# Relation stage: two chunks a step, rows stacked by the kind of the source node

## The reference

```python
h = jnp.maximum(_layernorm(x, axis=-1), 0.0)
# weight: 8 bases of 64 x 64; w_comp: 16 relations x 8 bases
# relation of an edge = (edge type, kind of source, kind of target): 4 * 2 * 2
# out[dst] += h[src] @ (sum over b of w_comp[relation, b] * weight[b]);  + bias
x = x + _L2_gnn_ref(h, node_type_2, src, dst, edge_type_4, weight, w_comp, bias)
```

## Time and profile before

| what | value |
|---|---|
| median of 3 runs | 9735.94 us (9728.96 to 9739.63) |
| profiled execution | 9729.18 us, span 9727.4 us |
| VectorE, TensorE, GpSimd, ScalarE busy in the span | 72%, 64%, 46%, 28% |
| relation block, first gather to the end of its block | 6232.5 to 7149.5 us |

### The profile page before, as it was taken

One profiled execution on the slowest core, in us unless ns is written; L12 is line 12 of the kernel. 1 busy time (PEld: TensorE's weight loads), 2 busy tenths in 40 slices (PEclk: granted clock), 3 DMA queues, 4 the chain that ended last, 5 costly groups with the idle time before them and its releaser, 6 DMA issues. The chain is left out here.

```text
span 9727.4 us, 105611 instructions
## 1 busy us (share of the span) xinstructions
PE 6247.1 (64%) x15818; PEld 3037.1 (31%) x15818; DVE 6982.1 (72%) x21830; ACT 2708.9 (28%) x6469; POOL 4476.3 (46%) x4367
## 2 busy tenths in 40 slices
PE   0006999996999996774001998899979999900000
PEld 0002333333444444663000556533323333300000
DVE  2666887785666666886556997799979999887522
ACT  0002333331111112554332000122224444346300
POOL 1775555554555553554552000144446666413466
PEclk9998555555666665555555995699965555555555
DMA  4002334342222221112332004444433333323222
GB/s 144 1 1 42 56 55 57 56 55 48 47 47 47 47 47 25 38 36 55 89 89 57 3 1 124 123 100 101 100 73 74 75 73 75 72 93 111 83 81 79
DMA packets 937155, 627.22 MB, mean 64 GB/s; under 512 B 639609, under 2 KB 801942, under 8 KB 935568
## 3 DMA queue, kind: packets, MB, share of 16 engines
q1 hardware_dynamic: 579396, 305.26, 12.3%
q0 software_dynamic: 137984, 138.92, 10.9%
q10 hardware_dynamic: 219656, 181.82, 5.7%
HBM read 431.05 MB, written 227.84 MB: 68 GB/s over the span
## 5 line engine op out<-in xcount | busy, mean ns | idle before, releaser
L707 POOL DMA_INDIRECT a_xg<-t_XL,a_ix x784 | 790.0, 1008 | 688.2 <-issue 653.2
L707 POOL DMA_INDIRECT b_xg<-t_H,b_ix x784 | 776.6, 991 | 666.6 <-PE b_bank L917 378.5
L1737 POOL DMA_INDIRECT f_dg<-t_D,f_ix x392 | 370.6, 945 | 1498.2 <-DMA f_ix<-t_PSRC 1402.2
L707 POOL DMA_INDIRECT g_xg<-t_D,g_ix x784 | 824.0, 1051 | 493.4 <-issue 225.5
L1090 POOL DMA_INDIRECT t_RANK<-m_place,m_at x392 | 385.6, 984 | 409.0 <-DMA m_place<-t_POS 301.8
L1275 POOL DMA_INDIRECT l_d<-t_D,l_ix x392 | 370.7, 946 | 405.4 <-DVE l_xs L1291 238.0
L1365 PE MATMUL pr_prow<-c_ident,pr_col 128*1 128x128 f32 x2 | 0.6, 396 | 789.9 <-DVE pr_col L1383 789.9
L2135 POOL DMA_INDIRECT out<-o_y,o_ix x392 | 388.8, 992 | 225.4 <-issue 184.3
L428 POOL DMA_INDIRECT t_XL<-ix_pv,ix_si x392 | 407.9, 1041 | 159.4 <-issue 130.3
L745 DVE TENSOR_TENSOR b_zt<-b_xl,b_bank 128x512 f32<-128x512 f32 x98 | 67.4, 687 | 537.4 <-PE b_bank L936 237.3
L1324 ACT ACTIVATE l_hn<-l_xs,l_sm 128x64 f32<-128x64 f32 x784 | 265.0, 426 | 505.6 <-DVE l_sm L588 283.9
(11 more groups left out here) (437 smaller groups left out, 17260.9 us busy)
## 6 DMA issues: line engine op xcount, KB each, us to landing
t_XL<-in_nodes ACTq DMA_DIRECT2D x10, 2578.1 KB
t_XSD<-a_xg SPq DMA_DIRECT2D x98, 256.0 KB
t_H<-a_oE ACTq DMA_DIRECT2D x98, 256.0 KB
l_xb<-t_XSD SPq DMA_DIRECT2D x49, 512.0 KB
f_rl<-t_REL SPq DMA_DIRECT2D x98, 256.0 KB
g_xb<-t_XSD SPq DMA_DIRECT2D x98, 256.0 KB
n_x<-in_x SPq DMA_DIRECT2D x39, 640.0 KB
out<-n_y ACTq DMA_DIRECT2D x39, 640.0 KB
```

The costliest lines, as they stand in the source:

```text
L707: nc.gpsimd.indirect_dma_start(xg[k][:, j, i, :], None, table, bass.IndirectOffsetOnAxis(ap=ix[k][:, i, j:j + 1], axis=0)).then_inc(s_g[k] ...
L1737: nc.gpsimd.indirect_dma_start(dg[k][:, j, :], None, T["D2"], bass.IndirectOffsetOnAxis(ap=ix[k][:, j:j + 1], axis=0)).then_inc(s_g[k], 16)
```

## The change

A step takes two chunks, 1024 edges, and there are 49 (`NB`). The kind of the source node is told apart by rows: `positions_block` no longer adds it to the number of the relation but stores it as T["KS"]. norm splits scale and shift into two pairs, one multiplied by the kind, the other by one less the kind (`by_kind`); normed then writes each row twice, once in columns 0 to 63 and once in 64 to 127, and the ReLU leaves zeros in the half that isn't the edge's. Turned, that is 128 rows. The two kinds' weights lie above each other in c_wft, so f_v takes two products of 128 rows for 512 edges where it took four of 64, and f_sel and f_m come in twos as well. The four banks of f_v now hold two halves of a step, f_m has one bank for each half, and turn and turn back keep one bank each: both halves pass through the one turn bank in turn.

Loads, gathers, sums, copies and norm factors are of 1024 edges, with four slots for what comes in up to f_hn and two for the rest. VectorE's list is result 5, select 3, sums 4, norm 1. TensorE's is vectors of the first half 3, compose of the first half 4, the same for the second half, turn 2, turn back 4. SyncE's relations have lag 2. The diff, cut to its core; of a function changed throughout only the new lines stand, since the old ones are printed above:

```diff
-            n += load(C["wflat"][:, :, :], a["L2_gnn_weight"].rearrange("b i o -> (b i o)").rearrange("(q p i) -> p q i", p=P, i=D))
+            for q in range(4):
+                n += load(C["wflat"][:, q % 2, q // 2, :],
+                          a["L2_gnn_weight"].rearrange("b i o -> (b i o)").rearrange("(q p i) -> q p i", p=P, i=D)[q])
...
+            sp.dma_start(full(T["KS"]), ks[:, :]).then_inc(s_st, 16)
+            sp.wait_ge(s_st, 32)
...
-            ch(v.scalar_tensor_tensor(part[:, :], kind[0][:, :], 8.0, et[:, :], ALU.mult, ALU.add))
-            v.scalar_tensor_tensor(rel[:, :], kind[1][:, :], 4.0, part[:, :], ALU.mult, ALU.add).then_inc(s_done, 1)
-            ch.done()
+            v.tensor_copy(ks[:, :], kind[0][:, :])
+            v.scalar_tensor_tensor(rel[:, :], kind[1][:, :], 4.0, et[:, :], ALU.mult, ALU.add).then_inc(s_done, 1)
...
-            for q in range(4):
-                last = nc.tensor.transpose(pf[:, q, :], C["wflat"][:, q, :], C["ident"][:, :])
+            for q in range(2):
+                last = nc.tensor.transpose(pf[:, q, :], C["wflat"][:, q, :, :].rearrange("p c i -> p (c i)"), C["ident"][:, :])
...
+        SL = 4
+        NB = NCH // 2
+        G = 2 * J
+        four, two = range(SL), range(2)
+        hn = [m.sb(f"hn{k}", [P, 2, J, 2, D]) for k in four]
+        hT = [m.sb(f"hT{k}", [P, 2, CH]) for k in two]
+        rl = [m.sb(f"rl{k}", [P, 2, CH]) for k in two]
...
+        by_kind = m.sb("bykind", [P, 2, 2, G])
         b_turn = m.ps("turn", [P, CH])
+        b_v = [[m.ps(f"v{u}{g}", [P, CH]) for g in two] for u in two]
+        b_m = [m.ps(f"m{u}", [P, CH]) for u in two]
+        b_back = m.ps("back", [P, 2, J, D])
...
+                    sp.wait_ge(s_g[k], 16 * G * q)
+                sp.dma_start(ix[k][:, :, :], words_of_two(T["PSRC"], n)).then_inc(s_ix[k], 16)
+                if old:
+                    sp.wait_ge(s_f, n - SL + 1)
+                for u in two:
+                    sp.dma_start(xb[k][:, u, :, :], rows_of_two(T["XSD"], n)[:, u, :, 0:D]).then_inc(s_xb[k], 16)
+                sp.dma_start(ks[k][:, :, :], words_of_two(T["KS"], n)).then_inc(s_xb[k], 16)
...
+                if later(n, 2):
                     sp.wait_ge(s_sel, 4 * (n - 1))
...
+                    sp.wait_ge(s_ag, 2 * (n - 1))
...
-            flow(sp, [(0, load), (4, before), (3, keeps), (1, relations)])
+            flow(sp, [(0, load), (4, before), (3, keeps), (2, relations)], total=NB, slots=SL)
...
+                for u in two:
+                    for j in range(J):
+                        nc.gpsimd.indirect_dma_start(
+                            dg[k][:, u, j, :], None, T["D2"],
+                            bass.IndirectOffsetOnAxis(ap=ix[k][:, u, j:j + 1], axis=0)).then_inc(s_g[k], 16)
+            flow(pool, [(0, gather)], total=NB, slots=SL)
...
+                dve.wait_ge(s_g[k], 16 * G * (q + 1))
+                dve.wait_ge(s_xb[k], 48 * (q + 1))
+                if old:
+                    dve.wait_ge(s_hn, n - SL + 1)
+                v.tensor_tensor(xs[k][:, :, :, :], dg[k][:, :, :, :], xb[k][:, :, :, :], ALU.add).then_inc(s_xs, 1)
                 dve.wait_ge(s_xs, n + 1)
+                ch(row_moments(nc, flat(xs[k][:, :, :, :]), bn))
+                norm_factors(nc, ch, bn, sm, s_n)
+                dve.wait_ge(s_n, n + 1)
                 if later(n):
                     dve.wait_ge(s_hn, n)
+                of_source = ks[k][:, :, :].rearrange("p u j -> p (u j)").unsqueeze(1).to_broadcast([P, 2, G])
+                ch(v.tensor_tensor(by_kind[:, 1, :, :], sm[:, 4:6, :], of_source, ALU.mult))
+                v.tensor_tensor(by_kind[:, 0, :, :], sm[:, 4:6, :], by_kind[:, 1, :, :], ALU.subtract).then_inc(s_f, 1)
                 ch.done()
...
+                dve.wait_ge(s_rl[k % 2], 16 * counted(n, k, q))
+                for u in two:
+                    if later(n, 2):
+                        dve.wait_ge(s_m, 2 * (n - 2) + u + 1)
+                    for g in two:
+                        dve.wait_ge(s_v, 4 * n + 2 * u + g + 1)
+                        v.scalar_tensor_tensor(sel[k % 2][u][g][:, :], rl[k % 2][:, u, :], C["relp"][:, g:g + 1], b_v[u][g][:, :],
+                                               ALU.is_equal, ALU.mult).then_inc(s_sel, 1)
...
+                dve.wait_ge(s_kp[k % 2], 16 * counted(n, k, q))
+                if later(n, 2):
                     dve.wait_ge(s_b, n - 1)
+                for u in two:
+                    dve.wait_ge(s_m, 2 * n + u + 1)
+                    before = ag[1 - k % 2][:, 1, CH - 1:CH] if u == 0 else ag[k % 2][:, 0, CH - 1:CH]
+                    if u or later(n):
+                        dve.wait_ge(s_ag, 2 * n + u)
+                    v.tensor_tensor_scan(ag[k % 2][:, u, :], kp[k % 2][:, u, :], b_m[u][0:D, :], before,
+                                         ALU.mult, ALU.add).then_inc(s_ag, 1)
...
-            flow(dve, [(5, result), (4, sums), (1, norm), (2, select)])
+            flow(dve, [(5, result), (3, select), (4, sums), (1, norm)], total=NB, slots=SL)
...
+                for u in two:
+                    if u or later(n):
+                        hold(pe, s_pturn, (s_h, 2 * n + u))
+                    for j in range(J):
+                        last = nc.tensor.transpose(split(b_turn[:, :])[:, :, j],
+                                                   hn[k][:, u, j, :, :].rearrange("p c d -> p (c d)"), C["ident"][:, :])
+                    last.then_inc(s_t, 1)
+
+            def vectors(n, k, u):
+                pe.wait_ge(s_h, 2 * n + u + 1)
+                for g in two:
+                    if later(n):
+                        pe.wait_ge(s_sel, 4 * (n - 1) + 2 * u + g + 1)
+                    nc.tensor.matmul(b_v[u][g][:, :], C["wft"][:, g, :], hT[k % 2][:, u, :], start=True, stop=True).then_inc(s_v, 1)
+
+            def compose(n, k, u):
                 if later(n):
+                    pe.wait_ge(s_ag, 2 * (n - 1) + u + 1)
+                for g in two:
+                    pe.wait_ge(s_sel, 4 * n + 2 * u + g + 1)
+                    last = nc.tensor.matmul(b_m[u][0:D, :], C["cstk"][:, :], sel[k % 2][u][g][:, :],
+                                            start=(g == 0), stop=(g == 1))
                 last.then_inc(s_m, 1)
...
-            flow(pe, [(2, turn), (3, compose), (2, vectors), (4, turn_back)])
+            first_half, second_half = ((lambda n, k, q, old, fn=fn, u=u: fn(n, k, u)) for fn, u in ((vectors, 0), (vectors, 1)))
+            first_sum, second_sum = ((lambda n, k, q, old, u=u: compose(n, k, u)) for u in two)
+            flow(pe, [(3, first_half), (4, first_sum), (3, second_half), (4, second_sum), (2, turn), (4, turn_back)],
+                 total=NB, slots=SL)
...
+                    act.wait_ge(s_t, 2 * (n - SL + 1))
+                for g in range(G):
+                    for c in two:
+                        last = f(hn[k][:, g // J, g % J, c, :], xs[k][:, g // J, g % J, :], ACT.Relu,
+                                 bias=by_kind[:, c, 1, g:g + 1], scale=by_kind[:, c, 0, g:g + 1])
                 last.then_inc(s_hn, 1)
+                for u in two:
+                    act.wait_ge(s_t, 2 * n + u + 1)
+                    if later(n, 2):
+                        act.wait_ge(s_v, 4 * (n - 2) + 2 * u + 2)
+                    f(hT[k % 2][:, u, :], b_turn[:, :], ACT.Copy).then_inc(s_h, 1)
...
-            flow(act, [(2, turned), (1, normed), (5, store)])
+            flow(act, [(2, turned), (1, normed), (5, store)], total=NB, slots=SL)
```

More of the change, by code:

```diff
@@ L531, in positions_block @@
         kind = [m.sb(f"kind{i}", [P, EF], I32) for i in range(2)]
[L532 to L533 removed]
+        et, ks, rel = (m.sb(x, [P, EF]) for x in ("et", "ks", "rel"))
+        s_ld, s_done, s_st = (m.sem(x) for x in "ld done st".split())
         block = ctx.enter_context(nc.Block())
@@ L1687, in relation_block @@
-        d2b = [m.sb(f"d2b{k}", [P, J, D]) for k in two]
-        sel = [[m.sb(f"sel{k}{g}", [P, CH]) for g in range(4)] for k in two]
-        ag = [m.sb(f"ag{k}", [D, CH]) for k in two]
-        o = [m.sb(f"o{k}", [P, J, D]) for k in two]
+        SL = 4
+        NB = NCH // 2
+        G = 2 * J
+        four, two = range(SL), range(2)
+        ix = [m.sb(f"ix{k}", [P, 2, J], I32) for k in four]
+        dg = [m.sb(f"dg{k}", [P, 2, J, D]) for k in four]
+        xb = [m.sb(f"xb{k}", [P, 2, J, D]) for k in four]
@@ new lines, in relation_block @@
+        ks = [m.sb(f"ks{k}", [P, 2, J]) for k in four]
+        xs = [m.sb(f"xs{k}", [P, 2, J, D]) for k in four]
+        hn = [m.sb(f"hn{k}", [P, 2, J, 2, D]) for k in four]
+        hT = [m.sb(f"hT{k}", [P, 2, CH]) for k in two]
+        rl = [m.sb(f"rl{k}", [P, 2, CH]) for k in two]
+        kp = [m.sb(f"kp{k}", [D, 2, CH]) for k in two]
+        d2 = [m.sb(f"d2{k}", [P, 2, J, D]) for k in two]
+        d2b = m.sb("d2b", [P, 2, J, D])
+        sel = [[[m.sb(f"sel{k}{u}{g}", [P, CH]) for g in two] for u in two] for k in two]
```

(26 more changed lines are left out.)

125 lines of the change are left out of this document (40 added, 85 removed).

## The result

The changed kernel took 9577.47 us, median of 4 runs (9562.17 to 9591.02), beside 9737.78 for the kernel before: ratio 0.9837, 95% interval 0.9816 to 0.9858. That is 160 us less, where 233 were forecast: the time lies inside the range and the sign is right, but it is 74 us above the forecast of 9503. About 63 of these lie in the relation stage and 3 in the rest of the program; the last 9 come from the median, which is 15.3 us above the profiled execution, where 6.7 was assumed.

The account below looks back on a forecast made before the run. A two-step loop through ScalarE and TensorE with clock falls, 13.6 us a step, was to bound the relation stage: 85 + 44 x 13.6 = 683 us against 917, +1 around it, so 9503 us; range 9438 to 9618.

Parts of the forecast that it names:

- VectorE's terms: Relation stage, VectorE's pieces of one 1024-edge step: sum 12.17 us against 18.0 for two chunks, taken as 12.4.
- the factors are still 18 operations ... 3.95 + 0.61 = 4.56: VectorE's norm: eight statistics and 18 tiny, twice as wide factor operations cost 4.56 us a step, where two chunks paid 7.90.
- to 60: Start of the relation stage: fourth norm ends at 48 us, the fifth step does the whole 12.17, to 60.
- The loop: Two-step chain through ScalarE's activations, TensorE and VectorE's norm: 23.6 to 24.7 us at full clock, 27.1 with clock falls.
- the sign named for a failure: Forecast fails if normed activations end long before TensorE turns, so that the two-step loop does not set the step.
- a fall in almost every step: TensorE's clock falls in the thin stretch of over 5 us, costing the loop 1.5 to 4.3 us, taken as 2.9.
- rival 1: TensorE's clock holds, so VectorE bounds the relation stage at 12.4 us a step: stage 631, total 9451 us; chance 0.26.
- the forecast's window: Relation stage's step of 13.0 to 14.5 us, around the forecast of 13.6; chance 0.46.
- the reason I gave as decisive: Two-step loop over ScalarE's activations and TensorE, with clock falls, sets the step at 13.6 us.
- 90% or less: Sign of a right forecast: VectorE busy some 90% of the stage or less, gaps before f_sel or the scan.
- The turned weight load: TensorE's turned tile, 64 to 128 columns: 0.06 us a step by measured row; skill's rule would add 427 ns.
- the failed cover of the prediction: SyncE's indices not issued over a step ahead: GpSimd waits 4.5 us more, 14.5 us a step instead of 10.0.

Follow-up runs that it names:

- kernel without gathers: Changed kernel with a step's eight gathers replaced by two plain loads of rows in order on the same queue: 9449.79 us, ratio 0.9729.
- after: Profile of the changed kernel, unaltered, from its first measurement against the kernel before: 9577.47 us, ratio 0.9837.
- later gathers: Changed kernel with gathers of step n held until factors of step n-2 are ready: 9200.25 us, ratio 0.9724 (quicker chip); 9572.72 us, 0.9832 (slower).

## Why the prediction was right in sign and short in size

**VectorE's terms** held within 0.1 us each, waits aside, but for "the factors are still 18 operations ... 3.95 + 0.61 = 4.56" (with the statistics). They measured 6.19: 5.04 + 1.15. This is the step that failed: I took the price of a chained operation from the f stage, where the trace before is clean, and gave it no room for holes. The g block's rows in the same trace had some, but small: 3.3 and 4.3 us above clean for two lines, which is 0.08 us a chunk for six of the 18 operations, or 0.2 for all if alike (an estimate). They warned of the kind of loss, not of 1.6 us. The kernel without gathers has 1.46 us a step and 39 us at the start less, 108 in all by the ratio.

**The start**, "to 60", missed the holes of the first norms in the same way: 34 us.

**The loop.** Its order is right: in after the turns start 0.39 to 0.73 us behind the last activation in 39 of the 40 steps, so the sign named for a failure did not appear. Its length is nearly so; the 16 activations took 5.41 us instead of 5.84. On the quicker chip, with later gathers, TensorE in order of time:

```profile
6446.91 0.63 PE L1839 MATMUL f_turn<-c_ident,f_hn 128*128 128x128 f32 x4 [2.40 <-ACT f_hn L1883]
6448.41 1.09 PE L1839 MATMUL f_turn<-c_ident,f_hn 128*128 128x128 f32 x4 [0.86 <-ACT f_hT L1892]
6449.43 1.23 PE L1865 MATMUL f_back<-c_ident,f_ag 64*128 64x64 f32 x8
6450.58 3.78 PE L1848 MATMUL f_v<-f_hT,c_wft 128*128 128x512 f32 x4
...
6460.37 0.66 PE L1839 MATMUL f_turn<-c_ident,f_hn 128*128 128x128 f32 x4
6461.90 0.63 PE L1839 MATMUL f_turn<-c_ident,f_hn 128*128 128x128 f32 x4 [0.87 <-ACT f_hT L1892]
6462.46 1.17 PE L1865 MATMUL f_back<-c_ident,f_ag 64*128 64x64 f32 x8
6463.56 1.98 PE L1848 MATMUL f_v<-f_hT,c_wft 128*128 128x512 f32 x4
```

TensorE waits 2.40 for the activations and then 0.86 for the copy, as foretold. After that wait the granted clock is at half in one step (turns 1.09, f_v 3.78) and stays at full in the next (0.63, 1.98). I expected "a fall in almost every step" at 2.9. The price of one is near that: 0.46 on the turns and 1.80 on f_v here. But of the 40 steps 16 have a clock of 1.00, the other 24 of 0.76 to 0.87. Two periods of 12.78 are 25.6 us, against 24.7 for the loop at full clock with both pauses after f_m (24.3 with the measured activations), so the falls cost at most about 1.3 over two steps, not 2.9. Without holes rival 1's 12.4 a step was nearer than my 13.6.

**So two errors offset each other.** The clock was priced 0.8 us a step too high, the factors 1.6 too low. The period of after, 14.23, lies in the forecast's window (13.0 to 14.5), but by luck: the reason I gave as decisive isn't, since f_sel waits for f_v 3.2 us in 400 of after, the factors at least 36. VectorE is busy 75% as "90% or less" allows and the clock is 0.84, inside 0.7 to 0.85, but the gaps stand in the factors and not before f_sel or the scans.

**The turned weight load** grew by 0.03 us for four turns (0.60 to 0.63), 0.06 a step as by the row; the rule of the Trainium skill that the prediction quotes (TensorE: Matmul & The Clock Gate, LDWEIGHTS) would have given 0.43. One load in itself grew from 111 to 141 ns in the median, 0.24 us for eight, most of it beside the products.

**GpSimd and SyncE.** GpSimd waits for indices in 23 of some 28 steps in 6300:6700 of after, 109.1 us in all, 3.28 and 4.32 in two I looked at: the failed cover of the prediction; but no f_xs waits for a gather in the steady stretch, so it cost nothing.

**What stays open.** What the holes are. They need gathers in flight (shown on the slower kind: 36 us to 0.2, and on one chip factors of 5.15 to 3.40), don't follow bytes alone, and are absent on two of the four chips of the experiments. At the start one stands before a row statistic that waits for nothing, as if VectorE's instructions came late. In the steady stretch it is otherwise. Of the operations in the 40 steps that wait for nothing (seven row statistics a step and the second and third operation of the factors, 360) none has a hole over 0.1 us; all 102 of the factors' holes stand before operations that wait for a semaphore. The Trainium skill (Runtime: NRT & Kernel Launch, Instruction fetch mechanics) says that an engine's sequencer fetches its instructions itself in blocks by DMA, and calls that mostly hidden. The trace has such packets, 11 in 6300:6700, but from 6460 to 6915, some 32 steps of after, its queues are only these (queue: packets, MB, share):

```profile
q1 hardware_dynamic: 65498, 41.98, 37.0%
q0 software_dynamic: 8192, 8.40, 24.6%
q10 hardware_dynamic: 8704, 8.39, 5.3%
```

No packet of instructions is among them, while the factors' idle time is 47.6 us there, 1.5 a step. So as far as the trace records fetches, late fetching is not what makes the steady holes; for those of the start it stays possible. That GpSimd's own work blocks VectorE is no better supported: on the quicker chip GpSimd was busy 288 of 400 us without holes, and with gathers at most two steps ahead 691 of the 720 operations of the factors lay within a burst of gathers (pauses under 0.5 us counted in), and only 12 of them were late. What is left, a late signal of a semaphore or something the trace doesn't record, is not shown. The changed kernel itself was not run on the quicker kind; that it gains about 2.8% there rests on the one with later gathers.

## What to carry to other kernels

When a chain of tiny dependent operations is priced, look at its idle time in all stages with the same neighbours (here gathers), not only in the stage being changed, and widen the range where any of them has holes; their size after a change may be far larger, here 1.6 us a step where the other stage had about 0.2. When an edit shortens one wait, add up all waits of the engine before calling it gone: here holes moved from the factors to f_sel. And set a step beside the unaltered kernel on the same chip. Joining two chunks in a step is worth most where such a chain is paid once per step. When a saving makes VectorE lighter, look for the loop close behind: here 0.61 us saved on it gave 0.25.

## What the runs showed of the hardware

The same kernel takes 2.7 to 3.0% more on some chips: 9716 and 9746 against 9463 and 9464. The difference is not in the duration of single operations. The last block, which none of the kernels touches, has the same 392 indirect stores one by one, yet takes 585.7 us from first to last in after and 506.8 on the quicker chip:

```profile
L2177 POOL DMA_INDIRECT out<-o_y,o_ix x392: 969/972/1226, 8964.9 to 9550.6; - x196
```

```profile
L2177 POOL DMA_INDIRECT out<-o_y,o_ix x392: 971/972/1217, 8674.9 to 9181.7; - x196
```

On the slower chips a chained operation of VectorE starts 0.20 us after the one before it or, in a hole, 0.70 or 1.40 in about half of the cases (50 of 102); on the quicker ones it is about 0.20 throughout (in all of the g block, 0.4 us of surplus waits).
